# Attention on one Trainium2 core: two of four query tiles transposed by 32x32 squares on VectorE and moved by DMA, the other two on TensorE by pairs of chunks

## What is computed

```
q      = hidden @ Wq.T + bq                      # 4096 x 128
scores = q @ memory_keys.T / sqrt(128)           # 4096 x 4096
probs  = softmax(scores, axis=-1)
output = (probs @ memory_values) @ Wo.T + bo
```

## Time and profile before

| | us |
|---|---|
| median of 3 runs | 714.54 (713.49 to 715.75) |
| the profiled execution, its own time | 713.79 |
| its span, first to last instruction | 712.0 |
| feed-forward stage 1 and unit 0 | 0 to 131.7 |
| unit 1 | 131.7 to 163.0 |
| units 2 to 15 | 163.0 to 595.3 |
| the values-only step and the last projection | 595.3 to 622.5 |
| feed-forward stage 2 | 622.5 to 712.0 |

### The profile page before, as it was taken

One profiled execution on the slowest core, in us unless ns is written; L12 is line 12 of the kernel. 1 busy time (PEld: TensorE's weight loads), 2 busy tenths in 40 slices (PEclk: granted clock), 3 DMA queues, 4 the chain that ended last, 5 costly groups with the idle time before them and its releaser, 6 DMA issues.

```text
span 712.0 us, 10456 instructions
## 1 busy us (share of the span) xinstructions
PE 675.9 (95%) x3521; PEld 503.8 (71%) x3536; DVE 549.5 (77%) x1176; ACT 474.0 (67%) x893; POOL 121.9 (17%) x226
## 2 busy tenths in 40 slices
PE   3898988999999999999999999999999999989997
PEld 3444444788888888888888888888888888745542
DVE  3799876877876886787688677778867875799885
ACT  3577887757666756756666675666666665478886
POOL 4755412102000200200020020002001021242200
PEclk9899999999999999999999999999999999999999
DMA  7011100000000000000000000000000000000001
GB/s 279 2 46 44 59 30 0 1 1 0 1 2 1 1 0 1 1 1 1 0 1 1 1 0 1 1 1 1 0 1 1 1 1 0 1 1 30 31 16 44
DMA packets 4327, 10.87 MB, mean 15 GB/s; under 512 B 859, under 2 KB 1459, under 8 KB 4147
## 3 DMA queue, kind: packets, MB, share of 16 engines
q1 hardware_dynamic: 3987, 10.21, 4.2%
q10 hardware_dynamic: 288, 0.01, 0.0%
HBM read 8.12 MB, written 2.10 MB: 14 GB/s over the span
## 4 chain that ended last, share of the span: by engine, by line
PE 82%; DVE 8%; issue 4%; ACT 4%; POOL 1%; DMA 0%; ACTq 0%; DVEq 0%; POOLq 0%
PE banks L1088 15%; PE banks L1111 8%; PE banks L1110 8%; PE banks L1112 8%; PE banks L1073 8%; PE banks L1074 8%; PE banks L1075 8%; PE banks L953 4%; PE banks L962 3%; DVE probs L697 3%; PE banks L969 2%; PE banks L1120 2%; PE banks L909 2%; ACT probs L435 1%; PE banks L901 1%
## 5 line engine op out<-in xcount | busy, mean ns | idle before, releaser
L542 ACT ACTIVATE p_hi<-banks 128x512 fp32r<-128x512 f32 x256 | 154.0, 602 | 134.4 <-PE banks L1088 134.2
L784 DVE TENSOR_TENSOR p_lo<-banks,p_hi 128x512 fp32r<-128x512 f32 x256 | 176.2, 689 | 82.6 <-ACT p_hi L542 80.7
L821 DVE TENSOR_REDUCE bank_max<-banks 128x1 f32<-128x512 f32 x256 | 171.0, 686 | 30.2 <-PE banks L1075 26.4
L553 ACT ACTIVATE probs<-banks,neg_max 128x512 f32<-128x512 f32 (+1 forms) x192 | 158.8, 833 | 14.7 <-DVE neg_max L842 14.7
L1088 PE MATMUL banks<-ident,probs 128*128 128x128 f32 x1024 | 153.4, 272 | 1.4 <-DVE p_lo L784 1.4
L1088 PEld LDWEIGHTS banks<-ident,probs 128*128 128x128 f32 x1024 | 126.2, 140 | 36.5 <-issue 5.1
L1110 PE MATMUL banks<-p_hi,kv_lo 128*128 128x512 f32 x256 | 120.0, 469 | 0.6 <-DVE p_lo L784 0.6
L446 ACT ACTIVATE probs<-probs 128x1024 bf16<-128x1024 bf16 x96 | 92.1, 979 | 33.1 <-DVE probs L697 24.3
L697 DVE SCALAR_TENSOR_TENSOR probs<-banks,wbc 128x1024 bf16<-128x1024 f32 x80 | 95.4, 1218 | 22.5 <-PE banks L953 19.5
L1073 PE MATMUL banks<-kv_lo,q_parts 128*128 128x512 f32 x256 | 102.6, 401 | 1.2 <-issue 1.2
L1111 PE MATMUL banks<-p_lo,kv_hi 128*128 128x512 f32 x256 | 101.4, 396 | 0.0
(11 more groups left out here) (87 smaller groups left out, 708.4 us busy)
## 6 DMA issues: line engine op xcount, KB each, us to landing
kv_stage<-in_keys_values SPq DMA_DIRECT2D x8, 512.0 KB, 3.5
out<-X SPq DMA_DIRECT2D x8, 256.0 KB, 2.0
X<-in_x SPq DMA_DIRECT2D x1, 1280.0 KB, 9.2
X<-in_x SPq DMA_DIRECT2D x3, 256.0 KB, 5.3
probs<-in_wup SPq DMA_DIRECT2D x1, 704.0 KB, 5.2
probs<-in_wdown SPq DMA_DIRECT2D x1, 704.0 KB, 6.6
sup_s<-in_shared_up SPq DMA_DIRECT2D x1, 88.0 KB
sdown_s<-in_shared_down SPq DMA_DIRECT2D x1, 88.0 KB
```

Source lines behind the costliest of these rows:

```text
L542: act.activation(p_hi[:, c % 4, :], TB[c % 2][:, :], ACT.Copy).then_inc(p_hi_done, 1)
L553: act.activation(probs[:, v % 2, i, first * N:(first + count) * N], score_banks(u, i)[:, first:first + count, :].rearrange("p b n -> p (b ...
L784: dve.tensor_tensor(p_lo[:, c % 4, :], TB[c % 2][:, :], p_hi[:, c % 4, :].bitcast(fp32), ALU.subtract).then_inc(p_lo_done, 1)
L821: dve.tensor_reduce(bank_max[:, i % 2, q:q + 1], score_banks(u, i)[:, q, :], AX.X, ALU.max).then_inc(bank_max_done, 1)
```

## The change

Of the four tiles of a unit the first two are **moved**, the last two (**own**) stay on PE.

Moved tiles: ACT writes their exponentials to a new buffer `E2`, as four strips of 32 keys' width (strip `b` holds keys 32b to 32b+31 of each chunk). DVE transposes 32x32 squares in place (`transpose_squares`), half a tile (1024 elements a partition) at a time, four instructions a unit, in steps 1 and 2. SP then issues 16 transfers a unit, each from 32 partitions to 32 partitions, 2 rows of 2 KB a partition (128 KB), to `probsT`, two buffers in turn. ACT makes the high part from `probsT` (`moved_high`) and POOL, not DVE, the low part (`moved_low`).

Own tiles: PE transposes two chunks of two tiles into one bank (`transpose_pair`), so eight banks a unit and not sixteen; `own_high` on ACT and `own_low` on DVE follow for each pair. `p_hi` and `p_lo` become rings of three pairs; the moving operand of the value products is now 16 runs of 32 elements, 64 apart.

The value products run four chunks behind, not two; the last four fall into the step `UNITS + 1`. The maximum of banks 0 and 1 is one instruction. `E2` lies over `xT`, `xTb` and `wbc`; there is one `E2`, so the first exponential of a unit waits until the 16 transfers of the unit before have landed (`moved`). Projection and second merge go from step 0 to step 1, and the early layer norms of the second feed-forward stage are placed anew in the last three units.

```diff
+MOVED = 2
+SQ = 32
+QUADS = P // SQ
+HI_RING = 3
+UP = KC // 2
+VLAG = 4
+MAX_BANKS = ((0, 2), (2, 1), (3, 1))
...
+        E2 = sb("E2", [P, MOVED, QUADS, N], fp32)
+        xT = [xq[:, :]] + [E2[:, 0, c, :] for c in range(AHEAD)]
+        xTb = E2[:, 1, 0:2, :].bitcast(bf16).rearrange("p a n -> p (a n)").rearrange("p (r n) -> p r n", r=RING)
+        wbc = E2[:, 1, 2:4, :]
...
+        probs = sb("probs", [P, 2, GT - MOVED, BLOCK], fp32)
+        probsT = sb("probsT", [P, 2, MOVED * QUADS, KC, SQ], fp32)
...
+            for u in range(UNITS):
+                if u == 0:
+                    sp.wait_ge(z_done, GROUPS)
+                    sp.wait_ge(down_done, GROUPS * SLOTS)
+                wait(sp, moved_lo_done, UP * (u - 1))
+                sp.wait_ge(squares_done, 2 * MOVED * (u + 1))
+                for b in range(QUADS):
+                    for i in range(QUADS):
+                        sp.dma_start(
+                            probsT[b * SQ:(b + 1) * SQ, u % 2, :, :, :].rearrange("p (t i) c q -> p i t (c q)", t=MOVED)
+                            [:, i, :, :], E2[i * SQ:(i + 1) * SQ, :, b, :]).then_inc(moved, 16)
...
+            def moved_low(w, m):
+                ring = UP * w + m
+                pool.wait_ge(moved_hi_done, ring + 1)
+                pool.tensor_tensor(moved_part(p_lo, ring), moved_pair(w, m), moved_part(p_hi, ring).bitcast(fp32),
+                                   ALU.subtract).then_inc(moved_lo_done, 1)
...
+                    if has_values:
+                        moved_low(u - 1, 2 * i)
+                        moved_low(u - 1, 2 * i + 1)
...
-                def p_high(c):
-                    done = (u - 1) * KC + c
-                    act.wait_ge(probsT_done, done + 1)
-                    wait(act, pv_done, done - 3)
-                    act.activation(p_hi[:, c % 4, :], TB[c % 2][:, :], ACT.Copy).then_inc(p_hi_done, 1)
+                def own_high(m):
+                    ring = UP * (u - 1) + m
+                    act.wait_ge(probsT_done, ring + 1)
+                    wait(act, pv_done, 2 * (ring - HI_RING + 1))
+                    act.activation(own_part(p_hi, ring), own_squares(ring), ACT.Copy).then_inc(p_hi_done, 1)
+                def moved_high(m):
+                    ring = UP * (u - 1) + m
+                    if m == 0:
+                        act.wait_ge(moved, moves(u))
+                    wait(act, pv_done, 2 * (ring - HI_RING + 1))
+                    act.activation(moved_part(p_hi, ring), moved_pair(u - 1, m), ACT.Copy).then_inc(moved_hi_done, 1)
...
-                    if i == 0 and piece == 0:
-                        wait(act, probsT_done, (u - 1) * KC)
-                        if u == 1:
-                            act.wait_ge(z_done, GROUPS)
-                            act.wait_ge(down_done, GROUPS * SLOTS)
-                    act.activation(
-                        probs[:, v % 2, i, first * N:(first + count) * N],
-                        score_banks(u, i)[:, first:first + count, :].rearrange("p b n -> p (b n)"), ACT.Exp,
-                        bias=neg_max[:, v, i:i + 1], accum_out=row_sum[:, v, i, piece:piece + 1]
-                    ).then_inc(exp_done, 1)
+                    source = score_banks(u, i)[:, first:first + count, :]
+                    if i < MOVED:
+                        if piece == 0:
+                            wait(act, moved, moves(u))
+                            if u == 0:
+                                act.wait_ge(shared_up_done, GROUPS)
+                                act.wait_ge(up_done, GROUPS * SLOTS)
+                                act.wait_ge(weighted, GROUPS * SLOTS)
+                        strips = E2[:, i, :, :].rearrange("p b (c q) -> p c b q", q=SQ)
+                        act.activation(
+                            strips[:, first * QUADS:(first + count) * QUADS, :, :],
+                            source.rearrange("p k (c b q) -> p (k c) b q", b=QUADS, q=SQ), ACT.Exp,
+                            bias=neg_max[:, v, i:i + 1], accum_out=row_sum[:, v, i, piece:piece + 1]
+                        ).then_inc(exp_done, 1)
...
+                        own_high(2 * i)
+                        if i:
+                            moved_high(2 * i)
                         if prepares and i == 3:
                             q_high(g + 1, (v // 2 + 1) % 2)
                     if has_scores:
                         exponentials(i, 0)
                         exponentials(i, 1)
                     if has_values:
-                        p_high(4 * i + 2)
+                        if not i:
+                            moved_high(2 * i)
+                        own_high(2 * i + 1)
                     if has_scores:
                         exponentials(i, 2)
                     if has_values:
-                        p_high(4 * i + 3)
+                        moved_high(2 * i + 1)
...
-            def p_low(u, c):
-                done = (u - 1) * KC + c
-                dve.wait_ge(p_hi_done, done + 1)
-                wait(dve, pv_done, done - 3)
-                dve.tensor_tensor(p_lo[:, c % 4, :], TB[c % 2][:, :], p_hi[:, c % 4, :].bitcast(fp32),
+            def own_low(u, m):
+                ring = UP * (u - 1) + m
+                dve.wait_ge(p_hi_done, ring + 1)
+                dve.tensor_tensor(own_part(p_lo, ring), own_squares(ring), own_part(p_hi, ring).bitcast(fp32),
                                   ALU.subtract).then_inc(p_lo_done, 1)
+            def transpose_squares(u, i, h):
+                dve.wait_ge(exp_done, (u * GT + i) * len(EXP_PIECES) + 2 + h)
+                half = E2[:, i, :, h * N // 2:(h + 1) * N // 2]
+                dve.transpose(half, half).then_inc(squares_done, 1)
...
+                    first, count = MAX_BANKS[k]
+                    dve.wait_ge(scores_done, (u * GT + i) * BANKS + first + count)
+                    dve.tensor_reduce(bank_max[:, i % 2, k:k + 1],
+                                      score_banks(u, i)[:, first:first + count, :].rearrange("p b n -> p (b n)"),
+                                      AX.X, ALU.max).then_inc(bank_max_done, 1)
...
+                    if has_values and i:
+                        own_low(u, 2 * i - 1)
                     if has_scores:
+                        if 1 <= i <= MOVED:
+                            transpose_squares(u, i - 1, 0)
                         maximum(i, 0)
-                    if i == 0 and has_projection and has_values:
-                        p_low(u, -1)
-                    if i > 0 and has_values:
-                        p_low(u, 4 * i - 1)
+                        if 1 <= i <= MOVED:
+                            transpose_squares(u, i - 1, 1)
+                        maximum(i, 1)
+                    if has_values:
+                        own_low(u, 2 * i)
                     if has_scores:
-                        maximum(i, 1)
                         maximum(i, 2)
...
-            def transpose_probs(u, v, c):
-                done = (u - 1) * KC + c
-                if u == 1 and c < 3:
-                    pe.wait_ge(exp_done, GT * len(EXP_PIECES) - 2 + c)
+            def transpose_pair(u, v, m):
+                ring = UP * (u - 1) + m
+                if m in (0, 2, 4):
+                    pe.wait_ge(exp_done, u * GT * len(EXP_PIECES) - 2 + m // 2)
+                if ring == 0:
                     pe.wait_ge(kv_lo_done, KV)
-                elif c in (0, 4, 8):
-                    pe.wait_ge(exp_done, u * GT * len(EXP_PIECES) - 2 + c // 4)
-                wait(pe, p_lo_done, done - 1)
-                for t in range(GT):
-                    last = pe.transpose(TB[c % 2][:, t * P:(t + 1) * P],
-                                        probs[:, (v + 1) % 2, t, c * P:(c + 1) * P], ident[:, :])
+                if ring == 1:
+                    pe.wait_ge(exp_done, GT * len(EXP_PIECES) - 1)
+                wait(pe, p_lo_done, ring - 1)
+                for half in range(2):
+                    for t in range(GT - MOVED):
+                        c = 2 * m + half
+                        at_column = (half * (GT - MOVED) + t) * P
+                        last = pe.transpose(TB[ring % 2][:, at_column:at_column + P],
+                                            probs[:, (v + 1) % 2, t, c * P:(c + 1) * P], ident[:, :])
                 last.then_inc(probsT_done, 1)
-            def values(w, wg, wv, c):
-                done = w * KC + c
-                pe.wait_ge(p_lo_done, done + 1)
+            def values(w, c):
+                ring = (w * KC + c) // 2
+                if c % 2 == 0:
+                    pe.wait_ge(p_lo_done, ring + 1)
+                    pe.wait_ge(moved_lo_done, ring + 1)
...
-                o = OB[wv % 2][:, :]
-                pe.matmul(o, vl, p_hi[:, c % 4, :], start=(c == 0), stop=False)
-                pe.matmul(o, vh, p_lo[:, c % 4, :], start=False, stop=False)
```

(32 more changed lines are left out.)

254 lines of the change are left out of this document (138 added, 116 removed).

## The result

The changed kernel takes 712.66 us (median of 8 runs, 711.92 to 713.33) beside 715.16 for the kernel before in the same job (8 runs): ratio 0.9963, 95% interval 0.9951 to 0.9975. That is 2.5 us faster, where 34.5 were forecast. The span fell by 1.4 us, from 712.0 to 710.6.

The account below looks back on a forecast made before the run. The prediction took TensorE (PE), full in units 2 to 15, as the bound. Units -37.5, start +5, end -2 sum to -34.5 us: span 677.5, forecast time 680 us, outer range 663 to 716.

Parts of the forecast that it names:

- PE, 8 x 0.44 a unit: Units 2 to 15: PE loses 8 of 16 transpose banks at 0.44 us each, 3.5 us a unit.
- the 27.4: Units 2 to 15: PE's own work in us per unit after losing the transposes, down from 30.88.
- slow squares: Rival: DVE's square transposes run at half speed, 2.4 us instead of 1.22, total 738 us; chance 0.10.
- the strided operand: Rival: value products reading 16 runs of 32 elements slow by 0.045 us on each 0.233, eating the gain; chance 0.04.
- The chain: Attention steps: from PE's scores through DVE's maxima and squares to ACT's first exponential, 5.99 us into steps with squares.
- the prediction's own formula: Shortest step with squares, set by PE's wait for banks 2 and 3: 8.93 + 0.06 - 1.84 = 7.15 us.
- covered: Steps 0, 1 and 3 of a unit: PE's own work or early exponentials hide the DVE and ACT times, no wait.
- Transfers: Each unit's DMA from E2: 12 us, between bounds of 9.5 and 17, hidden.
- The slack of 15.2: Us between the end of a unit's squares and the next unit's first exponential, which overwrites E2.
- Start, +5: Units 0 and 1: added squares and the wait for transfers make unit 2 start 5 us later (+3 to +8).
- End, -2: Values-only step and last projection: 3.5 us less for transposes, 1.4 more for two chunks, so 2 us shorter.
- the rival of late transfers: Rival: transfers land later than 15.2 us and every unit waits; landing at 17 gives 710 us; chance 0.18.

Follow-up runs that it names:

- e6: Changed kernel with squares transposed behind the negated maximum and one 2 MB transfer over 128 partitions replacing the sixteen; output differs; 683.99 us.
- e3: Changed kernel without the square transposes, transfers started when tile 1's exponentials are written; output differs; 679.02 us.
- e4: Changed kernel with one 2 MB transfer on 128 partitions in place of the 16 transfers on 32 partitions; output differs; 708.85 us.
- e1: Changed kernel with DVE's squares moved from among the maxima to behind the step's negated maximum; 704.19 us, ratio 0.9833 to the kernel before.
- e5: Changed kernel with squares behind the negated maximum and the last four of sixteen transfers issued by ACT; 707.95 us, ratio 0.9900 to the kernel before.
- e12: Changed kernel with squares' first half before the double maximum, low part behind it, second half behind the negated maximum; 696.89 us, ratio 0.9747 to before.
- e13: Changed kernel with only ACT's order changed: a kept pair's second high part ahead of the step's second exponential; 696.83 us, ratio 0.9759 to before.
- e8: Changed kernel with squares behind the negated maximum and 16 transfers of 64 KB behind each tile's squares, 32 a unit; 756.04 us.

## Why the prediction was wrong, point by point

**PE, 8 x 0.44 a unit.** Right by the price: in the changed kernel too a bank of transposes takes 0.44 of PE's time, and there are half as many. No run reached the 27.4 in every unit; e6 comes to 28.07, e3 to 28.0, with short waits of PE in both.

**Durations.** Right: squares 1.231 us (1.22 taken), between squares and double maximum 1.16 (1.13 taken), POOL 1.289 (1.29), value products still 0.23 apart, so the rivals of slow squares and of the strided operand fell. The Trainium skill (Vector Engine (DVE) Microarchitecture Reference, section 3.8) says one element per cycle per lane for the transpose; 1231 ns for 1024 elements, hardly more than a maximum of the same size (1202 ns), don't speak against it; no row here gives the length of a cycle.

**The chain: the step that failed.** The prediction laid it out "from the start of PE's step" and let DVE begin the double maximum at 1.60, when PE's sixth matmul is through. It began at 310.45, which is 2.90 after PE's 307.55. Ahead of it DVE has a low part that was counted in its busy time but not in the chain, and that waits for ACT's high part, which in turn waits behind two exponentials of the step before. The squares' first half, which was taken to be done before 1.60, comes behind that low part too. So the first exponential came 7.23 us into PE's step (314.78 less 307.55), not 5.99; from the double maximum on the chain was right, 4.33 us where 4.39 were counted. PE begins its third bank of scores at 2.25 (309.80 less 307.55, 0.15 of it a wait; 1.84 was taken). Put into the prediction's own formula, 7.23 + 2.94 + 0.06 - 2.25 = 7.98, beside 8.07 measured, where it had 7.15. The formula looks at the third bank only. PE in fact stood first at the head of its step, 0.88 us for the first bank, until the first exponential had read it; the two waits are within 0.1 us of each other here. Step 1 was "covered" by PE's 7.4 and was not: it took 8.0 (299.58 to 307.55). Step 3 was "covered" too and took 7.0 (315.61 to 322.65), and 7.9 with the transposes for the next queries, where 6.5 and 6.9 were counted. The unit became 30.0 in place of 28.2: 14 x 1.8 = 25 of the 33 us that are missing.

The sign was there to be read: in the earlier trace rows DVE's low part has 20.5 us of idle time before it, 20.1 of them for ACT's high part. That row was used for its 689 ns alone. Before the change this wait cost nothing, since PE was full; the loop that it belongs to was the next bound.

**Transfers.** 12 us was right (12.1 in steady units, 12.5 at the start), but it had been chosen between two bounds and not summed: issues stand 0.64 apart and not 0.47, and each lands after 2.4 and not 2.0. The slack of 15.2 came out too (298.13 less 282.34 is 15.8), by terms that were off both ways: the squares end 5.2 us into PE's step 2 (277.10) and not 3.9, and step 3 was 1.0 longer. No steady unit waits, and e4 shows it. The margin was thinner than it looked: in e1 it was gone. The Trainium skill (SBUF - State Buffer, Door 1: The DMA port swizzle) has 189 GB/s for 32 partitions at 1 MiB. The Trainium skill (SBUF - State Buffer, "Can I just issue two DMAs to hit both halves?") has only 6% more for two transfers at once than for one, measured on tiles at partitions 0 and 64. Here one queue ran at 205 GB/s, above that figure, at the pace of its issues, and two queues in e5 at 220 to 227, 8 to 11% more. That is near what the skill has, but no run here shows that it is the ports which limit the second queue. Over 128 partitions 2 MB landed in 8.4 us (250 GB/s) in e6.

**Start, +5.** It was +10.1. The first exponential of unit 1 came at 147.67 (146 forecast), PE's tile 1 at 148.50 (146.8): +1.7. Then PE, idle for 6.2 us, had lost its clock. Windows of 1 us of the changed kernel:

```profile
146.00:147.00 1.00, 0.00 (x0) 0.00 (x0) 0.00 (x0) 0.00 (x0) 0.00 (x0) 0.66 0.77 176
147.00:148.00 1.00, 0.00 (x0) 0.00 (x0) 0.00 (x0) 0.33 (x1) 0.00 (x0) 0.50 0.00 0
...
152.00:153.00 1.00, 1.00 (x5) 0.81 (x4) 1.00 (x2) 0.68 (x2) 1.00 (x1) 0.50 0.00 0
153.00:154.00 1.00, 1.00 (x6) 0.82 (x5) 1.00 (x2) 0.44 (x1) 0.92 (x4) 0.93 0.00 0
```

It fell to the lower level, 1.2 GHz, while PE stood, and came back only in the slice from 153. Over 148.5 to 155 it is 0.64 in the mean: 6.5 x 0.36 = 2.3 us, an estimate, with PE busy all that time. The rest, 1.1, is in part rounding (163.0 less 139.5 is 23.5; 146.8 + 21.5 makes +5.3) and in part waits in the rest of unit 1, where PE stood 0.7 us from 155.00 to 173.06. The forecast priced the wait and not what follows it. e3 and e4, which have less to wait for, make the first copy of `oT` 5.2 and 3.5 us earlier.

**End, -2.** It was +0.8. Why is open: POOL's low parts were put beside PE's work at no cost, and of what is seen, PE waited 1.14 us for POOL's low part at 595.75, and 1.17 for ACT's last copy at 619.96. No run tested this.

**Rivals.** None of them was it; a loop of DVE and ACT set off by the low part at the head of the step was in none. The outer range, 663 to 716, held the time only because it was drawn to the rival of late transfers, whose cause is not what happened. That the change still came out faster, by 0.4% where the prediction gave 0.76 to more than 0.3%, is luck too: the loop happened to close 0.9 us below the old unit. e12 and e13 still stand 17 us above 680: both have the long start, e13 a unit in two of 29.3 us, and e12 a landing that is late by 0.3 to 1.6 us in eight of the units after unit 1.

## What to carry to other kernels

When the engine that is full is about to lose work, look for the loop that closes without it: follow each of the other engines from one step to the next through its program order and its waits, and sum it. An idle time with a releaser on an engine that isn't the bound is free today and is the first candidate for tomorrow's bound; a group's row shows both its duration and that idle time. Where to put added work on such an engine is a matter of what stands behind it: late for the chain, early for the transfer that depends on it, and half of each was as good as any place tried here. What an idle time is put down to isn't what it costs: where an instruction waits for two things, count from the other one.

## What was not expected of the hardware

- SP took 0.64 us per issue for transfers of 32 partitions (median 597 ns of each for 128 KB, 591 for 64 KB), against 0.47 for the loads at the kernel's start, so the rate went with the size of a piece: 205 GB/s and 103. On ACT's queue four of them stopped ACT for 2.24 us.
- 2 MB in sixteen pieces of 32 partitions land 12.1 us behind the first issue; in one piece over 128 partitions 8.4 (e6).
- A single wait of PE, 6.2 us long, cost by the estimate above 2.3 us more than its length, since the clock was at the lower level until 153 when work came again at 148.5. In e8 waits of up to 3.9 us a unit did the same; in the changed kernel's units 2 to 15, with waits of at most 2.2 us, it is 1.00 in the mean.
